# GpSimd's sums of the output weights in 256-column operations, and three of seven low parts moved from VectorE to GpSimd

## The chip, the cores and the metric

One core of one Trainium2 chip runs the whole program. The metric is the device time of one execution in microseconds; a kernel's time is the median of its runs.

## The reference

The block is x + attention(xn) w_o + ffn(xn), with xn the layer norm of x, for 4 sequences of 512 tokens of 1024 values. What the change touches is the output projection of the attention, whose input is 2048 tokens by 4096 values (32 heads of 128) and whose weight w_o is 4096 by 1024:

```
qkv = hidden_states @ w_qkv            # 32 query heads, 8 key and value heads of 128
attn = softmax(scores * scale + bias)  # causal, bias = -slope * sqrt(distance)
out  = einsum(attn, v).reshape(B, S, 32 * 128)
return out @ w_o                       # the stage of this case
```

## The kernel before

Every fp32 product is made of three matmuls of split numbers: an operand is stored as a high part (`_hi`, type fp32r) and a low part (`_lo`, the number less its high part), and `product` (L643) issues high by high (L645), high by low (L646) and low by high (L647). ScalarE makes high parts (`high`, L892), VectorE or GpSimd the low parts (`low`, L1127; GpSimd's own, L592).

The first half of the span projects q, k, v and the ffn and stores them in DRAM. The second, from about 1215 us, is a loop over 128 units of attention (a sequence and a head), 4 units to a set, 2 sets to a group, so 16 groups of 8 units. Four engines run the same loop, each with its own written-out order. In unit n TensorE does the scores of n, then the transposes and the attention product of unit n-1 (`scores`, `transposes`, `attend`), and between them three or four "fills": parts of the output projection of an earlier set.

The output projection of a set is a block product of 2 by 2 blocks with seven products in place of eight. Its 14 parts are 2 tiles of 7 steps. A step multiplies an activation operand (`op_hi`, `op_lo`) with a weight operand `wo[:, step]`, a high and a low plane of 128x1024. VectorE adds each result to `acc` (`add_fill`, L1395). A fill waits for its weight's low part in the first tile of a group (L853), for its activation's low part (L854), and, as two PSUM banks alternate, for the addition of the fill before the last (L856).

The weights of a group are made once, in the four units n = 8g+2 to 8g+5 (`making`). Steps 0, 1 and 6 are blocks as loaded into `wo_raw`; steps 4, 2, 3 and 5 are sums and differences that GpSimd makes in `wo_sums` (L595), one 128x1024 operation each: step 4 in unit 8g+2, step 2 in 8g+3, steps 3 and 5 in 8g+4. `OUT_SPLITS` says in which unit they are split: 0 and 1 in 8g+3, 2, 3 and 4 in 8g+4, 5 and 6 in 8g+5. ScalarE makes the high parts at the end of its unit (L1114), VectorE the low parts at the end of its own (L1446), so ahead of its `maxima` of the next unit. `maxima` (L1364) frees the score banks and gives ScalarE its first exponential. In units 8g+4 to 8g+7 `bias_of` (L1353) follows it on VectorE.

GpSimd also makes the sums of activation operands (`out_sum`, L586) and their low parts (`out_low`, L592), all in operations of 128x256. In unit 8g+5 (`at_once`) it makes two sums and the low parts of parts 1, 2 and 3, which TensorE uses in the same unit; ScalarE makes their high parts ahead of that unit's exponentials, and for part 2 waits for GpSimd's sum. SyncE loads the next group's `wo_raw` in unit 8g+7, after all low parts of this one (L435).

Of the kernel before, what the change touches and what calls it, by code (L numbers as in the profile page):

```python
# [7 lines left out]
ALU = mybir.AluOpType  # L8
ACT = mybir.ActivationFunctionType
AX = mybir.AxisListType  # L10
F32 = mybir.dt.float32
# [33 lines left out]
STEPS = 7  # L45
# [14 lines left out]

OUT_SPLITS = ((), (0, 1), (2, 3, 4), (5, 6))
WO_SUMS_IN = ((4,), (2,), (3, 5), ())
GROUPS = SETS // 2


def block_program(nc, x, w_all, w_o, w_ag, w_lora, gate_b, consts, out):
    with ExitStack() as ctx:
        base = 16512

        def at(name, offset, shape, dt=F32):  # L70
            return nc.alloc_sbuf_tensor_at(name, shape, dt, offset=base + offset)

        def sem(name):
            return ctx.enter_context(nc.semaphore(name))
# [45 lines left out]
        k = at("k", 8 * K, [P, 2, 2, SEQ], F32R)  # L120
# [9 lines left out]
        wo = at("wo", 76 * K, [P, STEPS, 2, 1024], F32R)  # L130
# [73 lines left out]
        s_wo_sum = sem("s_wo_sum")  # L204
        s_wo_hi = sem("s_wo_hi")
        s_wo_lo = sem("s_wo_lo")
        s_bias = sem("s_bias")
        s_scores = sem("s_scores")
        s_neg_max = sem("s_neg_max")
# [18 lines left out]
        def number(pr, m, st):  # L228
            return (pr * MATRICES + m) * STEPS + st
# [36 lines left out]
        def stores_h(pr, m, i):  # L266
            return stored_h(pr, m, i) + 16 * 3 * (4 * pr + (min(i, 4) if m == VALUES else 4))

        def stores_r(pr, m, i):
            return stored(pr, m, i) + 16 * 3 * (2 * pr + (min(i, 2) if m == VALUES else 2))  # L270
# [57 lines left out]
        def making(n):  # L328

            group, since = (n - 2) // (2 * G), (n - 2) % (2 * G)  # L330
            return (group, since) if n >= 2 and group < GROUPS and since < G else (None, None)

        def out_splits(n):

            group, since = making(n)
            return [] if group is None else [(group, i) for i in OUT_SPLITS[since]]

        def out_sums_in(n):

            group, since = making(n)  # L340
            return [] if group is None else [(group, i) for i in WO_SUMS_IN[since]]

        WO_SUMS = (4, 2, 3, 5)

        def summed(group, step):
            return len(WO_SUMS) * group + WO_SUMS.index(step) + 1

        def used(group, step):

            return PARTS * (2 * group - 1) + STEPS + step + 1  # L350

        def wo_source(step):

            return {0: wo_raw[0][:, :], 1: wo_raw[1][:, :], 6: wo_raw[3][:, :], 4: wo_raw[2][:, :],
                    5: wo_raw[1][:, :]}.get(step, wo_sum[:, step, 1])
# [4 lines left out]
        def _(sp):  # L360
# [51 lines left out]
            def out_block(group, i):  # L412

                half, pair = i // 2, i % 2
                head = group % KV_HEADS * G + 2 * pair
                sp.dma_start(wo_raw[i][:, :].rearrange("p (h c) -> p h c", h=2),
                             w_o[bass.ds(head * P, 2 * P), half * 512:(half + 1) * 512].rearrange("(h p) c -> p h c", p=P)
                             ).then_inc(s_wo_raw[i], 16)

            def out_weights(n):  # L420

                if n in (1, 2):
                    sp.wait_ge(s_bank, 4 * TOTAL)
                    for i in ((0, 2), (1, 3))[n - 1]:
                        out_block(0, i)
                if n in range(3, 7):

                    sp.wait_ge(s_store_h, stores_h(2, VALUES, 0))
                    sp.wait_ge(s_store_a, stores_r(2, VALUES, 0))
                    sp.wait_ge(s_store_b, stores_r(2, VALUES, 0))  # L430
                    for tt in ((0, 2), (1, 3), (4, 6), (5, 7))[n - 3]:
                        sp.dma_start(acc[:, tt, :], acc_s[bass.ds(tt * P, P), :]).then_inc(s_acc_in[tt], 16)
                group = n // (2 * G)
                if n % (2 * G) == G + 3 and group + 1 < GROUPS:
                    sp.wait_ge(s_wo_lo, STEPS * (group + 1))  # L435
                    sp.wait_ge(s_wo_sum, len(WO_SUMS) * (group + 1))
                    for i in range(4):
                        out_block(group + 1, i)
# [21 lines left out]
            for n in range(UNITS):  # L460
                pr, g, b, h = unit(n)
                s = n // G
# [24 lines left out]
        def _(pool):  # L487
# [107 lines left out]
            def wo_sums(group, step):  # L595

                a11, a12, a21, a22 = (r[:, :] for r in wo_raw)
                to, first, second, op = {4: (a21, a11, a21, ALU.subtract), 2: (wo_sum[:, 2, 1], a22, a21, ALU.subtract),
                                         5: (a12, a12, wo_sum[:, 2, 1], ALU.subtract),
                                         3: (wo_sum[:, 3, 1], wo_sum[:, 2, 1], a11, ALU.add)}[step]  # L600
                if step == 4:
                    pool.wait_ge(s_wo_raw[0], 16 * (group + 1))
                    pool.wait_ge(s_wo_raw[2], 16 * (group + 1))
                if step == 2:
                    pool.wait_ge(s_wo_raw[3], 16 * (group + 1))
                if step in (2, 3) and group:
                    pool.wait_ge(s_fill, used(group, step))
                elif step in (2, 3):
                    pool.wait_ge(s_bank, 4 * TOTAL)
                if step != 4:  # L610
                    pool.wait_ge(s_wo_sum, summed(group, 4 if step == 2 else 2))
                if step == 5:
                    pool.wait_ge(s_wo_lo, STEPS * group + 2)
                nc.gpsimd.tensor_tensor(to, first, second, op).then_inc(s_wo_sum, 1)

            for n in range(UNITS + G + 1):
                at_once, later = shaped(n)
                s, c = n // G - 1, n % G
                for group, step in out_sums_in(n) if c == 0 else ():
                    wo_sums(group, step)  # L620
                if c == 0 and at_once + later:
                    pool.wait_ge(s_at_raw, G * s + 2)
                    for tile, k in OUT_SUMS[0:2]:
                        out_sum(s, tile, k)
                if at_once:
                    pool.wait_ge(s_at_raw, G * (s + 1))
                    for tile, k in OUT_SUMS[2:4]:
                        out_sum(s, tile, k)
                for part in at_once:
                    out_low(*part)  # L630
                if at_once:
                    out_sum(s, *OUT_SUMS[4])
                if c == 2 and later:
                    for tile, k in OUT_SUMS[5:8]:
                        out_sum(s, tile, k)
                for part in later:
                    out_low(*part)
                for group, step in out_sums_in(n) if c != 0 else ():
                    wo_sums(group, step)

        @block.tensor
        def _(pe):
# [205 lines left out]
            def fill_in(s, tile, k):  # L848

                part = tile * STEPS + k  # L850
                f = PARTS * s + part
                if s % 2 == 0 and tile == 0:
                    pe.wait_ge(s_wo_lo, STEPS * (s // 2) + k + 1)  # L853
                pe.wait_ge(s_op_lo, f + 1)  # L854
                if f >= 2:
                    pe.wait_ge(s_acc, f - 1)  # L856
                for kt in range(2):
                    cols = slice(kt * 512, (kt + 1) * 512)
                    last = product(fill[f % 2][:, :], (op_hi[:, part, kt, :], op_lo[:, part, kt, :]),
                                   (wo[:, k, 0, cols], wo[:, k, 1, cols]), kt == 0 and k in STARTS, kt == 1)  # L860
                last.then_inc(s_fill, 1)
# [256 lines left out]
        def _(dve):  # L1118
# [278 lines left out]
            def out_split(group, step):  # L1397

                dve.wait_ge(s_wo_hi, STEPS * group + step + 1)
                if step == 2:  # L1400
                    dve.wait_ge(s_wo_sum, len(WO_SUMS) * (group + 1))
                low(wo[:, step, 1], wo_source(step), wo[:, step, 0], s_wo_lo)
# [10 lines left out]
            for pr in range(PAIRS):  # L1413
                operands(pr)
                for m in range(MATRICES):
                    for st in range(STEPS):
                        n = number(pr, m, st)
# [16 lines left out]
            for n in range(UNITS + G + 1):  # L1434
                todo = fills(n)
                if 1 <= n < UNITS:
                    maxima(n)
                for f in todo[:1]:
                    add_fill(*f)
                if 1 <= n <= UNITS:  # L1440
                    transposed(n - 1)
                if n < UNITS:
                    inverses(n)
                for f in todo[1:]:
                    add_fill(*f)
                for part in out_splits(n):  # L1446
                    out_split(*part)


def constants():  # L1450
# [40 lines left out]
```

## Time and profile before

| | us |
|---|---|
| median of 3 runs | 2588.23 (2588.20 to 2589.75) |
| the profiled execution | 2589.15 |
| its span | 2587.4 |
| TensorE matmuls busy | 2440.0 (94%) |
| VectorE busy | 1627.0 (63%) |
| ScalarE busy | 1440.8 (56%) |
| GpSimd busy | 842.5 (33%) |

The busy times are of the whole span. In a timeline row the columns are start, duration, engine, line, operation, operands with shapes and count; in brackets stands how long the engine was idle before it and what released it.

### The profile page before, as it was taken

To read this page: it belongs to the slowest core of one execution; us is meant where nothing else is said; L and a number is where in the kernel's file an instruction comes from. 1 tells how busy PE (TensorE), PEld (TensorE's weight loads), DVE (VectorE), ACT (ScalarE), POOL (GpSimd) and SP (SyncE) were. 2 spreads that over 40 slices of the span, in tenths; PEclk is the share of its full clock that TensorE was granted. 3 is DMA by queue.
4 is the path that set the end of the run, shared out by engine and by line. 5 is a ranking of instruction groups with operands and counts; after the bars stand their busy time and mean duration, and the time that the engine had idled before them with its cause. 6 is when DMAs were issued, how large, how long until landed. Compare 5 with 4: busy or idle time off the path is not lost.

```text
span 2587.4 us, 34927 instructions
## 1 busy us (share of the span) xinstructions
PE 2440.0 (94%) x12128; PEld 2059.5 (80%) x12128; DVE 1627.0 (63%) x2905; ACT 1440.8 (56%) x3131; POOL 842.5 (33%) x966
## 2 busy tenths in 40 slices
PE   5999999996999999998899999999999999999998
PEld 4787888885777888886788878887888878888787
DVE  6657455555757355564676677667766777667765
ACT  4432133334523133334777777777776777777774
POOL 3211000002221000001355455544554455544544
PEclk9999999998999999999999999999999999999999
DMA  4536354464355444546422323132335231332221
GB/s 148 179 131 222 114 209 157 159 221 166 119 167 195 146 150 175 195 157 229 165 101 84 117 98 115 66 115 98 115 131 187 102 111 59 122 115 98 81 99 74
DMA packets 94703, 355.25 MB, mean 137 GB/s; under 512 B 8874, under 2 KB 9018, under 8 KB 85569
## 3 DMA queue, kind: packets, MB, share of 16 engines
q1 hardware_dynamic: 62480, 233.43, 25.1%
q0 software_dynamic: 32048, 119.60, 13.3%
q8 instruction: 97, 1.59, 0.2%
q14 instruction: 78, 0.63, 0.1%
HBM read 235.02 MB, written 117.97 MB: 136 GB/s over the span
## 4 chain that ended last, share of the span: by engine, by line
PE 78%; DVE 10%; issue 6%; ACT 3%; DMA 1%; POOL 1%; SPq 0%; DVEq 0%; ACTq 0%; POOLq 0%
PE ps L645 25%; PE ps L646 24%; PE ps L647 24%; PE ps L832 4%; DVE wo L1127 3%; DVE probs L1364 2%; DVE acc L1395 2%; ACT res_hi L892 1%; DVE stats L1141 1%; ACT rows L921 1%; DVE w_lo L1127 0%; DVE res_b L1127 0%; DMA lora_lo<-lora_s 0%; DVE res_a L1217 0%; DVE res_a L1127 0%
## 5 line engine op out<-in xcount | busy, mean ns | idle before, releaser
L892 ACT ACTIVATE w_hi<-raw 128x1024 fp32r<-128x1024 f32 x196 | 207.0, 1059 | 560.3 <-PE ps L647 440.4
L1127 DVE TENSOR_TENSOR w_lo<-raw,w_hi 128x1024 fp32r<-128x1024 f32 x196 | 239.1, 1223 | 358.5 <-ACT w_hi L892 358.4
L1395 DVE TENSOR_TENSOR acc<-ps,acc 128x512 f32<-128x512 f32 x448 | 298.0, 686 | 228.6 <-issue 207.9
L645 PE MATMUL ps<-x_hi,w_hi 128*128 128x512 f32 x1120 | 436.5, 390 | 0.0
L646 PE MATMUL ps<-x_lo,w_hi 128*128 128x512 f32 x1120 | 436.0, 389 | 0.0
L647 PE MATMUL ps<-x_hi,w_lo 128*128 128x512 f32 x1120 | 435.8, 389 | 0.0
L645 PE MATMUL ps<-wo,op_hi 128*128 128x512 f32 x896 | 368.4, 411 | 69.2 <-DVE acc L1395 55.4
L1032 ACT ACTIVATE probs<-probs,neg_max 128x512 f32<-128x512 f32 (+3 forms) x512 | 283.4, 565 | 212.5 <-DVE neg_max L1364 212.5
L647 PE MATMUL ps<-wo,op_lo 128*128 128x512 f32 x896 | 357.5, 399 | 0.0
L646 PE MATMUL ps<-wo,op_hi 128*128 128x512 f32 x896 | 355.9, 397 | 0.0
L1364 DVE CUSTOM_DVE_ANT_0 probs<-ps,bias 128x512 f32<-128x512 f32 (+3 forms) x512 | 220.4, 485 | 96.0 <-PE ps L647 93.9
L645 PEld LDWEIGHTS ps<-wo,op_hi 128*128 128x128 f32 x896 | 170.4, 190 | 108.5 <-issue 82.7
L592 POOL TENSOR_TENSOR op_lo<-op_raw,op_hi 128x256 fp32r<-128x256 f32 x256 | 189.6, 751 | 198.9 <-ACT op_hi L892 188.7
L1046 ACT ACTIVATE probs<-probs,row_inv 128x128 f32<-128x128 f32 (+3 forms) x512 | 245.5, 555 | 9.8 <-DVE row_inv L1376 9.8
L647 PEld LDWEIGHTS ps<-x_hi,w_lo 128*128 128x128 f32 x1120 | 210.4, 188 | 44.0
L645 PEld LDWEIGHTS ps<-x_hi,w_hi 128*128 128x128 f32 x1120 | 210.4, 188 | 43.7
L646 PEld LDWEIGHTS ps<-x_lo,w_hi 128*128 128x128 f32 x1120 | 210.4, 188 | 43.2
L518 POOL DMA_DIRECT2D qk_s<-res_hi x40 | 30.1, 753 | 656.3 <-ACT res_hi L892 645.5
L592 POOL TENSOR_TENSOR op_lo<-at_raw,op_hi 128x256 fp32r<-128x256 f32 x192 | 140.6, 739 | 305.2 <-ACT op_hi L892 209.6
L892 ACT ACTIVATE pt_hi<-ps 128x512 fp32r<-128x512 f32 (+1 forms) x384 | 173.2, 523 | 98.5 <-PE ps L832 98.3
L1127 DVE TENSOR_TENSOR pt_lo<-ps,pt_hi 128x512 fp32r<-128x512 f32 (+1 forms) x384 | 206.5, 592 | 26.1 <-ACT pt_hi L892 26.1
L647 PEld LDWEIGHTS ps<-wo,op_lo 128*128 128x128 f32 x896 | 171.0, 191 | 38.8
(156 smaller groups left out, 4997.3 us busy)
## 6 DMA issues: line engine op xcount, KB each, us to landing
raw<-w_all SPq DMA_DIRECT2D x70, 1024.0 KB, 5.2
q<-qk_s SPq DMA_DIRECT2D x128, 512.0 KB, 3.3
qk_s<-res_hi POOLq DMA_DIRECT2D x40, 1024.0 KB, 4.6
wo_raw<-w_o SPq DMA_DIRECT2D x64, 512.0 KB, 5.7
qk_s<-res_a POOLq DMA_DIRECT2D x20, 1024.0 KB, 9.1
qk_s<-res_b POOLq DMA_DIRECT2D x20, 1024.0 KB, 5.3
k<-qk_s SPq DMA_DIRECT2D x32, 512.0 KB, 5.8
v<-v_s SPq DMA_DIRECT2D x32, 512.0 KB, 7.9
```

The lines of the kernel that those rows point to most:

```text
L518: pool.dma_start(qk_s[b, first:first + 4, :, level, :].rearrange("h p c -> p h c"), source).then_inc(signal, 16)
L592: nc.gpsimd.tensor_tensor(op_lo[:, part], op_source(s, part), op_hi[:, part].bitcast(F32), ALU.subtract).then_inc(s_op_lo, 1)
L645: pe.matmul(to, st_hi, mv_hi, start=start, stop=False, skip_group_check=True)
L646: pe.matmul(to, st_hi, mv_lo, start=False, stop=False, skip_group_check=True)
L647: return pe.matmul(to, st_lo, mv_hi, start=False, stop=stop, skip_group_check=True)
L832: last = pe.transpose(to[:, c * P:(c + 1) * P], probs[:, n % 2, OFF[i] + j * P:OFF[i] + (j + 1) * P], ident[:, :])
L892: nc.scalar.activation(to, source, ACT.Copy).then_inc(signal, 1)
L1032: nc.scalar.activation(tile, tile, ACT.Exp, bias=neg_max[:, i:i + 1], scale=-1.0, accum_out=row_sum[:, i:i + 1]).then_inc(s_exp, 1)
L1046: last = nc.scalar.activation(tile, tile, ACT.Copy, scale=row_inv[:, i:i + 1])
L1127: nc.vector.tensor_tensor(to, source, high.bitcast(F32), ALU.subtract).then_inc(signal, 1)
L1364: nc.vector.tensor_tensor_reduce(out=probs[:, n % 2, OFF[i]:OFF[i] + (i + 1) * P], in0=score_bank[i], in1=bias[:, h, SEQ - (i + 1) * P:SEQ ...
L1395: nc.vector.tensor_tensor(to, fill[f % 2][:, :], to, ALU.add).then_inc(s_acc, 1)
```

## The change

`wo_sums` makes each sum in four operations of 256 columns, and signals after the last. The low parts of the weight operands 4, 5 and 6 are made by GpSimd, also in four operations each, at the end of its unit (after that unit's activation work), with a semaphore of their own, `s_wo_low`. VectorE keeps 0 to 3. TensorE and SyncE wait for the semaphore that fits.

```diff
+BY_POOL = (4, 5, 6)
+BY_DVE = STEPS - len(BY_POOL)
...
-                    sp.wait_ge(s_wo_lo, STEPS * (group + 1))
+                    sp.wait_ge(s_wo_lo, BY_DVE * (group + 1))
+                    sp.wait_ge(s_wo_low, len(BY_POOL) * (group + 1))
...
                 if step == 5:
-                    pool.wait_ge(s_wo_lo, STEPS * group + 2)
-                nc.gpsimd.tensor_tensor(to, first, second, op).then_inc(s_wo_sum, 1)
+                    pool.wait_ge(s_wo_lo, BY_DVE * group + 2)
+                for i in range(4):
+                    cut = slice(i * 256, (i + 1) * 256)
+                    last = nc.gpsimd.tensor_tensor(to[:, cut], first[:, cut], second[:, cut], op)
+                last.then_inc(s_wo_sum, 1)
+
+            def out_split(group, step):
+
+                pool.wait_ge(s_wo_hi, STEPS * group + step + 1)
+                for i in range(4):
+                    cut = slice(i * 256, (i + 1) * 256)
+                    last = nc.gpsimd.tensor_tensor(wo[:, step, 1, cut], wo_source(step)[:, cut],
+                                                   wo[:, step, 0, cut].bitcast(F32), ALU.subtract)
+                last.then_inc(s_wo_low, 1)
...
                 for group, step in out_sums_in(n) if c != 0 else ():
                     wo_sums(group, step)
+                for group, step in out_splits(n):
+                    if step in BY_POOL:
+                        out_split(group, step)
...
                 if s % 2 == 0 and tile == 0:
-                    pe.wait_ge(s_wo_lo, STEPS * (s // 2) + k + 1)
+                    if k in BY_POOL:
+                        pe.wait_ge(s_wo_low, len(BY_POOL) * (s // 2) + k - BY_DVE + 1)
+                    else:
+                        pe.wait_ge(s_wo_lo, BY_DVE * (s // 2) + k + 1)
...
-                for part in out_splits(n):
-                    out_split(*part)
+                for group, step in out_splits(n):
+                    if step not in BY_POOL:
+                        out_split(group, step)
```

## Rows read from the trace of the kernel before

**Rows 1.** The page: busy time of each engine; the chain that ended last, by engine.
```profile
PE 2440.0 (94%) x12128; PEld 2059.5 (80%) x12128; DVE 1627.0 (63%) x2905; ACT 1440.8 (56%) x3131; POOL 842.5 (33%) x966
...
PE 78%; DVE 10%; issue 6%; ACT 3%; DMA 1%; POOL 1%; SPq 0%; DVEq 0%; ACTq 0%; POOLq 0%
```

**Rows 2.** Waits, 1390 to 2587 us: waiter, releaser: us in total, times, longest.
```profile
PE ps L645 <- DVE acc L1395: 51.4, 27, 3.3
```

**Rows 3.** Timeline of TensorE: rows with idle time before them, and one group's transposes.
```profile
1763.13 0.47 PE L645 MATMUL ps<-wo,op_hi 128*128 128x512 f32 x1 [2.09 <-issue]
...
2093.27 0.77 PE L645 MATMUL ps<-wo,op_hi 128*128 128x512 f32 x1 [3.29 <-DVE acc L1395]
...
2101.34 1.25 PE L832 MATMUL ps<-ident,probs 128*128 128x128 f32 x10
2103.42 0.47 PE L645 MATMUL ps<-wo,op_hi 128*128 128x512 f32 x1 [0.83 <-issue]
...
2115.98 0.47 PE L645 MATMUL ps<-wo,op_hi 128*128 128x512 f32 x1 [0.53 <-DVE acc L1395]
```

**Rows 4.** Timeline of VectorE in the same group, from the end of unit 8g+3.
```profile
2084.90 4.84 DVE L1127 TENSOR_TENSOR wo<-wo_raw,wo 128x1024 fp32r<-128x1024 f32 x2
...
2091.42 1.10 DVE L1353 TENSOR_SCALAR bias<-dist,slopes 128x512 f32<-128x512 f32 x1
...
2097.67 2.36 DVE L1127 TENSOR_TENSOR wo<-wo_sum,wo 128x1024 fp32r<-128x1024 f32 x2 [0.72 <-ACT wo L892]
...
2110.38 2.68 DVE L1127 TENSOR_TENSOR wo<-wo_raw,wo 128x1024 fp32r<-128x1024 f32 x2
```

**Rows 5.** The first two alone, by form, around 2085 and 2089: busy us, mean ns.
```profile
L1127 DVE TENSOR_TENSOR wo<-wo_raw,wo 128x1024 fp32r<-128x1024 f32 x1 | 1.5, 1507 | 0.0
...
L1127 DVE TENSOR_TENSOR wo<-wo_raw,wo 128x1024 fp32r<-128x1024 f32 x1 | 3.4, 3405 | 0.0
```

**Rows 6.** Tile wo, all groups: ns shortest/median/longest, first and last start.
```profile
L1127 DVE TENSOR_TENSOR wo<-wo_sum,wo x32: 1216/1222/1227, 1248.9 to 2522.0; 128x1024 fp32r<-128x1024 f32 x32
```

**Rows 7.** Timeline of GpSimd in the same group.
```profile
2082.91 2.42 POOL L614 TENSOR_TENSOR wo_sum<-wo_raw,wo_raw 128x1024 f32<-128x1024 f32 x1
2085.48 3.19 POOL L614 TENSOR_TENSOR wo_sum<-wo_sum,wo_raw 128x1024 f32<-128x1024 f32 x1
2089.89 2.35 POOL L614 TENSOR_TENSOR wo_raw<-wo_raw,wo_sum 128x1024 f32<-128x1024 f32 x1 [1.23 <-DVE wo L1127]
...
2100.09 2.55 POOL L586 TENSOR_TENSOR op_raw<-at_raw,op_raw 128x256 f32<-128x256 f32 x2 [5.01 <-ACT at_raw L892]
2102.59 0.73 POOL L592 TENSOR_TENSOR op_lo<-at_raw,op_hi 128x256 fp32r<-128x256 f32 x1
...
2117.68 1.43 POOL L592 TENSOR_TENSOR op_lo<-at_raw,op_hi 128x256 fp32r<-128x256 f32 x2 [6.83 <-PE ps L647]
...
2127.34 0.74 POOL L592 TENSOR_TENSOR op_lo<-at_raw,op_hi 128x256 fp32r<-128x256 f32 x1
2128.03 0.74 POOL L592 TENSOR_TENSOR op_lo<-op_raw,op_hi 128x256 fp32r<-128x256 f32 x1
```

**Rows 8.** Timeline of ScalarE in the same group.
```profile
2094.76 1.92 ACT L1046 ACTIVATE probs<-probs,row_inv 128x128 f32<-128x128 f32 x4 [0.56 <-DVE row_inv L1376]
...
2098.49 1.05 ACT L892 ACTIVATE wo<-wo_raw 128x1024 fp32r<-128x1024 f32 x1
...
2101.85 0.72 ACT L892 ACTIVATE op_hi<-op_raw 128x256 fp32r<-128x256 f32 x2 [1.33 <-POOL op_raw L586]
...
2108.61 2.00 ACT L892 ACTIVATE wo<-wo_raw 128x1024 fp32r<-128x1024 f32 x2
```

**Rows 9.** Busy time by window; after POOL's comes the granted clock.
```profile
2094.00:2097.00 3.00, 3.00 (x11) 2.37 (x10) 2.00 (x5) 2.44 (x6) 0.73 (x1) 0.62 0.00 0
```

**Rows 10.** Timeline of SyncE's DMA queue in the same group.
```profile
2113.10 1.92 SPq L416 DMA_DIRECT2D wo_raw<-w_o  x4
2115.06 0.57 SPq L470 DMA_DIRECT2D k<-qk_s  x1
```

More of the change, by code:

```diff
@@ L206, in block_program @@
         s_wo_lo = sem("s_wo_lo")
+        s_wo_low = sem("s_wo_low")
         s_bias = sem("s_bias")
```

## The prediction

> **What bounds the kernel now.** I read the page first (busy times, then the chain), the waits of the attention half, and then the timelines of one group's four weight units on all engines. The page shows TensorE busy for 94% of the span and on 78% of the chain, VectorE on 10% [rows 1]. So the question is only where TensorE stands idle. The waits give one large item, TensorE on VectorE's addition, 51.4 us after 1390 us [rows 2]. The timeline of TensorE places it [rows 3]: in each group it idles at three places. A, in unit 8g+4: 3.29 us (14 groups; the last has 2.16, the first none of this kind). B, in 8g+5: 0.83 us. C, in 8g+6: 0.53 us. In the other five units the work is TensorE's own, so a group's period changes only by what happens between A and C.
>
> A comes from VectorE. The low parts of weights 0 and 1 take 4.84 us [rows 4], 1507 and 3405 ns [rows 5], where undisturbed ones take 1222 [rows 6]. Each ends 1.2 us after a GpSimd sum ends: GpSimd's step 2 runs 2082.91 to 2085.33, step 3 2085.48 to 2088.67 and itself takes 3.19 instead of about 2.4 [rows 7]. The two engines take turns, an instruction at a time. VectorE's bias (1.10 us) then ends just after GpSimd's step 5 does (2092.24) [rows 4, 7]; the addition behind it releases TensorE at 2093.27 [rows 3].
>
> A to B is always 10.15 us (2093.27 to 2103.42), and it is not TensorE's. VectorE's delay holds ScalarE, whose high part 4 ends at 2099.54 [rows 8]. GpSimd makes two activation sums (2100.09 to 2102.64), ScalarE waits 1.33 us for the first, and the low part of part 1 ends at 2103.32, when TensorE starts [rows 3, 7, 8]. TensorE's own work has slack there, which hides a low clock: after A it is granted 0.62 of its clock, 1.2 GHz for much of the stretch (2094 to 2097) [rows 9]. In 13 of 15 groups it is low for some 3 us or more after A. In the two where it isn't, B shows 2.1 us idle in place of 0.6 to 0.8 in nine groups (one in between, none visible in three) [rows 3]. So a low stretch costs about 1.3 to 1.5 us, up to 2.1, and B swallows it today. From B to C TensorE has no such slack.
>
> **The sums in pieces.** GpSimd's 128x256 operations are 0.74 us each but start 0.69 apart (2127.34, 2128.03) [rows 7]. Four are 2.8 us against 2.4, +0.4 for each of four sums. Steps 4 and 2 end with time to spare. What is gained is at A. The first low part arrives at 2084.90, as the third piece ends; it runs to 2086.15 instead of 2086.41. The fourth piece takes its turn (0.6 us), the second low part ends at 2087.87 instead of 2089.74: 1.87 earlier. The bias then waits for one piece of step 3, 0.2 us instead of 0.6. So VectorE is 2.2 to 2.3 us earlier, and TensorE's wait shrinks from 3.29 to about 1.0. Bounds: nothing, if VectorE can't get in between adjacent pieces, to 2.7, all of the 4.84 - 2.43 and more of the bias. I take 2.2, because the row at 2100.09 (two 256-column operations in 2.55 us beside a VectorE low part) shows turns after single operations.
>
> The Trainium skill, "SBUF — State Buffer", section "Who interferes with whom", says that a VectorE instruction with two SBUF inputs contends with GpSimd's reads, and that who issues first keeps the shared ports for the whole instruction. By that the piece length is what VectorE waits for; by a shared bandwidth it would gain nothing and the group would lose 2.2 us more. The trace agrees with the first (3405 ns beside one 2.4 us sum).
>
> ScalarE's normalise (2094.76) waits for VectorE, so it and the three high parts behind it move by 2.2, and high part 4 ends at 2097.34, call it T [rows 8]. Its other input, step 3, ends by 2091.0.
>
> **Low part 4 on GpSimd.** On VectorE it goes away behind 2 and 3, which run 2.36 us from T-1.87 before [rows 4]. That time isn't late there: what is late at B is GpSimd. GpSimd has the new work in its path: it waits for T, then 4 x 0.7 = 2.8 us, and only then the two sums (1.4 us) and the low part of part 1 (0.7 us), in program order. Two collisions come on top: step 5 ends about 2093.9, so the low part of part 0 delays VectorE's low parts 2 and 3, and the latter holds the port until T+0.8 (0.65 us more than without); the bias takes 0.4 during the pieces. TensorE then starts part 1 at T + 0.15 + 2.8 + 0.65 + 0.4 + 2.1 + 0.12 = T+6.2 = 2103.57. Before it was T+3.88. B costs 2.35 us against 2.2 gained: +0.15 against 2103.42. Without the collisions it would be -0.9, with the bad end at A +2.4. ScalarE's wait for the sum, 1.33 us, grows to some 3.7 and delays the unit's first exponential by 0.25.
>
> **The clock after B.** TensorE works 7.7 us at full clock between its release at A and the end of the transposes (2093.27 to 2102.59 less 1.6 lost to the low clock). Released at 2091.0 it is done at 2098.7, then idles until 2103.57: 4.9 us, more than the 3.29 after which the clock fell in 13 of 15. The low stretch now lies where nothing hides it. I take 1.5 us; bounds 0 (no fall) and 2.1 or a little more.
>
> **Low parts 5 and 6.** VectorE loses 2.68 us ahead of the maxima of unit 8g+6 [rows 4]; the idle at C goes, with the restart 0.6 us. GpSimd starts low part 5 after the high part (2108.61 + 1.05, now +0.25), ends it at 2112.85 and low part 6 at 2115.65, or 2116.05 with the bias between. TensorE wants number 6 at 2115.5 if its clock stayed up, at about 2117 if it fell: in the forecast the wait costs nothing, otherwise it is late next by up to 0.6 us. GpSimd's next work, sums and low parts for unit 8g+7, starts 3.5 us later and meets 6.83 us of idle in that queue [rows 7]. SyncE waits for all low parts: the weight loads and the load of k behind them, at 2113.10 [rows 10], go 3 us later; k is for unit 8g+8, whose scores come after all of 8g+7's work, and the weights for 8g+10. Hidden.
>
> **Sum.** A loaded group: +0.15 + 1.5 - 0.6 = +1.05 us. Fifteen of them: +15.8. The first group's sums ran before its low parts (nothing to gain but the bias), so it pays B almost whole: +2. Together +18. The profiled execution of 2589.15 us would be 2607, the median of 2588.23 so 2606.
>
> **Rivals.** (1) The clock stays up, or low part 6 eats the difference: +0.15 - 0.6, and up to 0.6 of wait back, 0 us a group, 2588 to 2592. For it: two groups of 15 kept their clock after 3.29 us. Against: 4.9 us is longer. (2) Faster: GpSimd's work at B meets no collision (VectorE's low part 3 finishes first, the bias falls elsewhere), -0.9 in place of +0.15, and the clock stays up or falls briefly: -0.8 a group, 2576. For it: all my times at B come from a phase of 0.5 us. Against: low part 3 starts after high part 3 and must last 1.2 us, past T. (3) Much slower: VectorE isn't let in between adjacent pieces at A. Then sum 2 and 3 hold it as before and 0.4 longer, and B's 2.35 stands unpaid: +2.4 + 0.4 + 1.5 - 0.6 = +3.7 a group, 2644. It decides from the first low part's duration: over 2 us says so. Against it stands the row at 2100.09, and only the reverse case (VectorE's turn) is well seen. The Trainium skill speaks against the change: "Perfetto Trace Analysis", section "Optimizing Scalar/DVE Operations", says that moving work between VectorE and GpSimd might not help, for their shared port. Here that is the collision term, 1.05 us a group at B; no row shows these pieces themselves.
>
> **Chances.** Forecast 0.53 (2596 to 2624, by the bounds of the clock and of half a microsecond at A and B), rival 1 0.16, rival 2 0.20, rival 3 0.11. A measurement tells 0.2% (5 us) from no change. Slower: forecast and rival 3, 0.64; same: most of rival 1, 0.14; faster: rival 2 and the rest, 0.22. The range reaches into rivals 1 and 2 below and stops short of rival 3: 2577 to 2627.
>
> **What would show it.** Low parts 0 and 1 together near 3.0 us (over 4.5: rival 3). TensorE's idle at A near 1, at B near 4.5 to 5, and a granted clock of about 0.6 just behind B and none low behind A. ScalarE waiting 3 to 4 us for a sum in unit 8g+5. GpSimd's low part 4 in 2.8 to 3.9 us. Idle at C gone. The forecast is wrong if B's idle is under 3 us, or if the clock stays up behind it.

## The result, and the profile after

The changed kernel takes 2602.64 us (median of 5 runs, 2600.86 to 2603.92) against 2588.56 (5 runs, 2588.20 to 2590.07) for the kernel before on the same chip: ratio 1.0052, 95% interval 1.0038 to 1.0067. It is slower by 14 us; forecast were 18. The profiled execution took 2603.18 us, its span is 2601.2, 13.8 longer than before.

The page of the changed kernel, busy times and then the chain by engine, beside [rows 1]:

```profile
PE 2444.5 (94%) x12128; PEld 2066.1 (79%) x12128; DVE 1547.2 (59%) x2857; ACT 1443.5 (55%) x3131; POOL 1013.7 (39%) x1350
...
PE 88%; DVE 4%; issue 4%; ACT 2%; POOL 1%; DMA 1%; SPq 0%; DVEq 0%; ACTq 0%; POOLq 0%
```

VectorE is 80 us less busy and GpSimd 171 more. VectorE fell from 10% of the chain to 4%, yet the end came later.

The waits from 1390 us on (waiter, releaser: us in total, times, longest), to be read beside [rows 2]:

```profile
PE ps L665 <- issue: 60.1, 15, 4.4
...
PE ps L665 <- DVE acc L1418: 11.6, 14, 0.9
```

TensorE's wait for VectorE's addition, A, shrank from 51.4 us to 11.6. In its place stand 60.1 us with no releaser named, 15 times: B, once in each of the 15 loaded groups (those behind the first). The timeline of TensorE in the group of [rows 3] (idle time before a row in brackets):

```profile
2099.75 0.47 PE L665 MATMUL ps<-wo,op_hi 128*128 128x512 f32 x1 [0.88 <-DVE acc L1418]
...
2106.50 1.25 PE L852 MATMUL ps<-ident,probs 128*128 128x128 f32 x10
...
2111.86 0.77 PE L665 MATMUL ps<-wo,op_hi 128*128 128x512 f32 x1 [4.11 <-issue]
2112.42 0.63 PE L666 MATMUL ps<-wo,op_hi 128*128 128x512 f32 x1
```

A idles 0.88 us instead of 3.29. From A to B it is 12.11 us instead of 10.15, with 4.11 us of idle in it. No row of C has idle time any more. Behind B the matmuls of 512 columns take 0.6 to 0.8 us and not 0.39. VectorE in the same group (the low parts of steps 0 and 1, the bias, the low parts of steps 2 and 3, the next bias), beside [rows 4]:

```profile
2093.80 2.93 DVE L1150 TENSOR_TENSOR wo<-wo_raw,wo 128x1024 fp32r<-128x1024 f32 x2
...
2098.40 0.60 DVE L1376 TENSOR_SCALAR bias<-dist,slopes 128x512 f32<-128x512 f32 x1
...
2104.15 2.54 DVE L1150 TENSOR_TENSOR wo<-wo_sum,wo 128x1024 fp32r<-128x1024 f32 x2 [1.76 <-ACT wo L915]
...
2108.36 0.57 DVE L1376 TENSOR_SCALAR bias<-dist,slopes 128x512 f32<-128x512 f32 x1
```

GpSimd, beside [rows 7]: the sums for steps 2, 3 and 5, the low part of step 4, and behind it the activation sums and low part on which TensorE waits at B:

```profile
2091.82 3.82 POOL L621 TENSOR_TENSOR wo_sum<-wo_raw,wo_raw 128x256 f32<-128x256 f32 x4
2095.79 3.79 POOL L621 TENSOR_TENSOR wo_sum<-wo_sum,wo_raw 128x256 f32<-128x256 f32 x4
2099.54 2.83 POOL L621 TENSOR_TENSOR wo_raw<-wo_raw,wo_sum 128x256 f32<-128x256 f32 x4
...
2106.09 3.43 POOL L629 TENSOR_TENSOR wo<-wo_raw,wo 128x256 fp32r<-128x256 f32 x4 [1.62 <-ACT wo L915]
2109.48 1.59 POOL L591 TENSOR_TENSOR op_raw<-at_raw,op_raw 128x256 f32<-128x256 f32 x2
2111.03 0.73 POOL L597 TENSOR_TENSOR op_lo<-at_raw,op_hi 128x256 fp32r<-128x256 f32 x1
```

ScalarE, beside [rows 8]: high part 4, and the activation's high parts after the wait for GpSimd's sum.

```profile
2104.97 1.04 ACT L915 ACTIVATE wo<-wo_raw 128x1024 fp32r<-128x1024 f32 x1
...
2110.30 0.72 ACT L915 ACTIVATE op_hi<-op_raw 128x256 fp32r<-128x256 f32 x2 [3.29 <-POOL op_raw L591]
```

So B is a chain through three engines: ScalarE ends high part 4 at 2106.01, GpSimd's low part 4 follows to 2109.52, two sums and one low part to 2111.76, and TensorE starts at 2111.86.

Two windows of 3 us, behind A and behind B (columns as in [rows 9]; the granted clock follows POOL's time). The kernel before had 0.62 behind A [rows 9] and the full clock behind B.

```profile
2099.80:2102.80 3.00, 3.00 (x16) 2.46 (x16) 2.58 (x6) 2.96 (x11) 3.00 (x5) 1.00 0.00 0
2111.90:2114.90 3.00, 3.00 (x7) 2.44 (x8) 1.84 (x5) 3.00 (x11) 1.96 (x4) 0.50 0.02 5
```

The low stretch has moved from behind A to behind B: 0.50 of the clock is the 1.2 GHz level. The clock fell behind B in all 15 loaded groups. In 8 of them the 3 us from B on were granted 0.50, as here. In the other 7 they were granted 0.61 to 0.69, because the fall came later. From 1300 us on, 140 matmuls of 512 columns take over 0.55 us; before it was 90.

A group lasted 84.7 to 84.95 us before (start to start of its first low part; once 85.77). Now it lasts 85.0 us where 7 or 8 of those matmuls ran at the low level, and 85.6 to 86.0 where 11 or 12 did; once 87.75, with 2.48 us of idle before scores that waited for q:

```profile
1967.97 0.47 PE L665 MATMUL ps<-k,q 128*128 128x512 f32 x1 [2.48 <-issue]
```

The kernel before in the same unit:

```profile
1960.09 0.47 PE L645 MATMUL ps<-k,q 128*128 128x512 f32 x1 [0.78 <-issue]
```

Up to the first loaded group the kernel loses 2.5 us, over 14 group periods 9.6 (0.69 each), and behind the last 1.7: together 13.8.

### The profile page after: what moved, and what is told of

It is laid out like the page before. It is cut to its first block, busy times and chain, and to the rows that moved or that the text cites. A ratio compares the mean times of both kernels' runs of the same rounds, so it can differ in the third digit from the quotient of the medians.

```text
span 2601.2 us, 35263 instructions
## 1 busy us (share of the span) xinstructions
PE 2444.5 (94%) x12128; PEld 2066.1 (79%) x12128; DVE 1547.2 (59%) x2857; ACT 1443.5 (55%) x3131; POOL 1013.7 (39%) x1350
## 4 chain that ended last, share of the span: by engine, by line
PE 88%; DVE 4%; issue 4%; ACT 2%; POOL 1%; DMA 1%; SPq 0%; DVEq 0%; ACTq 0%; POOLq 0%
PE ps L665 28%; PE ps L666 27%; PE ps L667 27%; PE ps L852 5%; DVE stats L1164 1%; ACT rows L944 1%; ACT res_hi L915 1%; DVE w_lo L1150 0%; DVE acc L1418 0%; DMA k<-qk_s 0%; DVE res_a L1240 0%; DVE res_a L1150 0%; DVE res_b L1240 0%; PE ps L747 0%; ACT w_hi L915 0%
## 5 line engine op out<-in xcount | busy, mean ns | idle before, releaser
L665 PE MATMUL ps<-wo,op_hi 128*128 128x512 f32 x896 | 374.6, 418 | 78.0 <-issue 61.7
L667 PE MATMUL ps<-wo,op_lo 128*128 128x512 f32 x896 | 363.8, 406 | 0.0
L666 PE MATMUL ps<-wo,op_hi 128*128 128x512 f32 x896 | 363.4, 406 | 0.0
```

What stands on the lines that cost most here:

```text
L665: pe.matmul(to, st_hi, mv_hi, start=start, stop=False, skip_group_check=True)
L666: pe.matmul(to, st_hi, mv_lo, start=False, stop=False, skip_group_check=True)
L667: return pe.matmul(to, st_lo, mv_hi, start=False, stop=stop, skip_group_check=True)
```

## The experiments

The theory: the pieces gain at A; low part 4 loses more at B, because GpSimd's activation work stands behind it in the same queue, and because TensorE's longer idle there is followed by the low clock. The first rival: the pieces are themselves a loss or nothing, and moving VectorE's work pays. The second: the loss is the engines' contention, wherever the low parts stand. All ratios are to the kernel before, which took about 2589.7 us on each chip used here and 2588.56 beside the changed kernel. So a difference of plain times between one of these kernels and the changed one can be off by about 1 us.

**pieces: the sums in pieces, no low part moved.**

```diff
-BY_POOL = (4, 5, 6)
+BY_POOL = ()
```

SyncE's wait on `s_wo_low`, which then nobody signals, goes too.

> Only the sums in 256-column pieces; all seven low parts stay on VectorE. Theory (pieces earn at A, low part 4 on GpSimd spends it at B, the clock behind B costs the rest): idle at A 0.9 us, A to B again 10.1 to 10.2 us, idle at C still about 0.5, so 2.4 us a loaded group: 2552 us if the clock stays up behind B, about 2575 if it falls there. Rival (the pieces themselves cost, by more issue and more turns): 2588 us or above.

Measured: 2560.83 us, ratio 0.9889 (0.9873 to 0.9906). TensorE at A, B and C of one group:

```profile
1661.14 0.47 PE L664 MATMUL ps<-wo,op_hi 128*128 128x512 f32 x1 [0.87 <-DVE acc L1417]
...
1671.15 0.47 PE L664 MATMUL ps<-wo,op_hi 128*128 128x512 f32 x1 [2.00 <-issue]
...
1683.95 0.47 PE L664 MATMUL ps<-wo,op_hi 128*128 128x512 f32 x1 [0.33 <-DVE acc L1417]
```

A has the 0.87 us of the changed kernel, from A to B it is 10.01 us (before 10.15), and only 29 slow matmuls are left. The half of the change that gains is this one: 29 us. It lies between the two values expected, since the clock fell behind B in 4 of the 14 groups whose B idles 2.0 us. Before, B's idle was shorter only because the low clock behind A filled it.

**moved_whole: the low parts moved, the sums as before.**

```diff
-                for i in range(4):
-                    cut = slice(i * 256, (i + 1) * 256)
-                    last = nc.gpsimd.tensor_tensor(to[:, cut], first[:, cut], second[:, cut], op)
-                last.then_inc(s_wo_sum, 1)
+                nc.gpsimd.tensor_tensor(to, first, second, op).then_inc(s_wo_sum, 1)
```

> Only the move of low parts 4, 5 and 6 to GpSimd; the sums stay whole. Theory: idle at A 3.3 us as before, A to B 12.1 us, idle at B near 3 us with a low clock behind it in many groups: +2.0 +1.0 to 1.6 -0.6 a group, 2625 to 2634 us. Rival (the pieces cost, the move is neutral): 2585 to 2592 us.

Measured: 2621.83 us, ratio 1.0125 (1.0110 to 1.0140). A and B:

```profile
1504.53 0.47 PE L662 MATMUL ps<-wo,op_hi 128*128 128x512 f32 x1 [3.29 <-DVE acc L1415]
...
1516.46 0.70 PE L662 MATMUL ps<-wo,op_hi 128*128 128x512 f32 x1 [3.90 <-issue]
```

A is as before and A to B is 11.9 to 12.0 us: the loss at B has nothing to do with the pieces of the sums. The moved low parts alone cost 32 us, the pieces alone gain 29. The two do not add up to the change's +14; on top of the pieces the move costs 42. What differs most is where the clock falls: with A's long idle kept, the clock fell behind A in 12 of the 14 groups with that idle. Where it fell there alone, B idles 1.3 to 2.5 us, which takes up the low stretch, and the group lasts 86.1 to 86.4 us. In 5 of the 14 the clock fell behind B, and all but one of those groups last 87.2 (the other has a long idle before scores). In the changed kernel it falls behind B every time. A fall behind B in many groups was expected here too, and the time is 3 us below that range.

**pieces_56: as changed, but low part 4 stays on VectorE.**

```diff
-BY_POOL = (4, 5, 6)
+BY_POOL = (5, 6)
```

> The change, but low part 4 goes back to VectorE; 5 and 6 stay on GpSimd. Theory: A 0.9 us, A to B near 10.2 us, C's idle gone: 3 us a group less than before, 2543 us with the clock up, up to 2566 if it falls behind B. Rival (low parts 5 and 6, with the loads of SyncE behind them, are what costs): no better than 2595 us.

Measured: 2555.90 us, ratio 0.9870 (0.9855 to 0.9884), 46.7 us below the changed kernel, from one low part of the three. A to B is 10.01 us again, C has no idle, 16 matmuls are slow. Low parts 5 and 6 gain, about 5 us (the intervals of the two kernels just overlap, but a group lasts 81.97 us against 82.4 to 83.6 in "pieces"); low part 4 alone does the harm. Against the second rival: the moved instructions are of one kind and contend alike, and two of three gain. One row spoils some of it (the clock fell behind it, and this group lasts 89.14 us):

```profile
1944.44 0.76 PE L665 MATMUL ps<-k,q 128*128 128x512 f32 x1 [4.19 <-issue]
```

**filled: the changed kernel with TensorE kept busy while it waits at B.** Ahead of the wait 16 more matmuls (`FILLER`) of 512 columns run on key tiles, and their results are used nowhere.

```diff
+                if s % 2 == 0 and part == 1:
+                    if f >= 2:
+                        pe.wait_ge(s_acc, f - 1)
+                    keys = key_sets[:, (s + 1) % 2, 0, :]
+                    for _ in range(FILLER):
+                        pe.matmul(fill[f % 2][:, :], keys[:, 0:P], keys, start=True, stop=True,
+                                  skip_group_check=True)
```

> The changed kernel, with 16 matmuls of 128x512 on key tiles put ahead of TensorE's wait at B, into a bank that the next fill starts anew; their results are used nowhere. Theory: TensorE is busy through most of the 4.1 us, the clock stays at 2.4 GHz behind B, 1.6 to 2.2 us a group less, of which the wait for low part 6 takes back up to 0.6: 2577 to 2588 us. Rival (the clock is a symptom, C is bound by GpSimd's low parts 5 and 6): unchanged, 2600 to 2604 us.

Measured: 2581.80 us, ratio 0.9971 (0.9959 to 0.9983), 20.8 us below the changed kernel although TensorE does more. TensorE at B, and the window behind it:

```profile
2096.11 3.90 PE L880 MATMUL ps<-k 128*128 128x512 f32 x16
2100.53 0.47 PE L666 MATMUL ps<-wo,op_hi 128*128 128x512 f32 x1 [0.52 <-issue]
```
```profile
2100.60:2103.60 3.00, 3.00 (x14) 2.48 (x15) 2.10 (x5) 3.00 (x11) 1.98 (x4) 1.00 0.00 0
```

The wait isn't shortened (A to B 12.18 us), only its consequence is gone: full clock behind B in every loaded group, and from 1300 us on no matmul of 512 columns over 0.55 us instead of 140. The window holds 14 matmuls; behind B of the changed kernel it held 7. The clock behind B costs 20.8 / 15 = 1.4 us a group. (The term was 1.5.)

**halves_512 and eighths_128: "pieces" with other sizes,** to see whether VectorE's turns go by the length of a piece.

```diff
-                for i in range(4):
-                    cut = slice(i * 256, (i + 1) * 256)
+                for i in range(2):
+                    cut = slice(i * 512, (i + 1) * 512)
```

> As 'pieces' (all low parts on VectorE), but the sums in two operations of 512 columns. Theory (VectorE waits out one GpSimd operation per turn): low parts 0 and 1 take near 3.9 us together, between 4.84 whole and 2.92 in pieces of 256, idle at A near 1.9 us, 2570 to 2576 us. Rival (VectorE gets in between any two operations at the moment it asks, the length doesn't matter): 2.9 us and 2561 us.

Measured: 2574.28 us, ratio 0.9940 (0.9925 to 0.9955), low parts 0 and 1 take 3.88 us (3.9 expected), idle at A is 2.22 us: between 3.29 (whole) and 0.87 (quarters). For the other, `range(8)` and slices of 128:

> As 'pieces', with eight operations of 128 columns. Theory: VectorE's turn comes a little sooner (2.7 to 2.8 us for the two), but each operation has a fixed cost, so a sum gets longer still: 2558 to 2566 us, no use beyond 256. Rival (the gain goes on in proportion): under 2555 us.

Measured: 2590.90 us, ratio 1.0010 (1.0001 to 1.0020). This is 25 us above the expected range; its ten runs spread from 2585.59 to 2599.57, and the trace is of the fastest. All groups of the tile wo_sum on GpSimd, and TensorE in unit 8g+5:

```profile
L620 POOL TENSOR_TENSOR wo_sum<-wo_sum,wo_raw x128: 450/459/647, 1221.7 to 2510.9; 128x128 f32<-128x128 f32 x128
```
```profile
1672.80 0.76 PE L664 MATMUL ps<-wo,op_hi 128*128 128x512 f32 x1 [3.19 <-DVE wo L1149]
```

A 128-column operation costs 0.46 us, not half of 0.74. A sum becomes 3.4 to 3.6 us, up to 5.4 with turns given away, and the weights' low parts come late (3.19 us of idle, on VectorE's). A itself was down to 0.78 us. Of the three lengths tried 256 is the best: below it the fixed cost of an operation eats what the turns gain.

**change_sync and p56_sync: SyncE's order.** In a unit, SyncE issues the group's weight loads, which wait for all low parts, ahead of the reads and writes of `acc`; q of the next unit is behind both. Both kernels exchange the two:

```diff
-                out_weights(n)
                 results(n)
+                out_weights(n)
```

> The changed kernel with one edit, SyncE's stores and reloads of the accumulator ahead of its wait for the low parts. Theory: the idle time of 2.48 us once in the half goes, and the one of the kernel before at the same place with it: 2.5 to 4 us less, 2599 us. It was left out of the prediction, which called SyncE's delay hidden. Rival: no difference.

> As 'pieces_56', with SyncE's stores and reloads of the accumulator ahead of its wait for the low parts. Theory: the one idle time of 4.19 us in the middle of the half (the change has 2.48 us there), which is a q load queued behind those reloads, goes: 3 to 4.5 us less than pieces_56, about 2552 us. Rival (it is DRAM or the stores themselves): no difference.

Measured: the change with it 2599.20 us, ratio 1.0034 (1.0022 to 1.0045), 3.4 us less than without; pieces_56 with it 2546.52 us, ratio 0.9837 (0.9822 to 0.9851), 9.4 less. The intervals of the first pair overlap and those of the second just don't, but in both traces the long idle before scores is gone. So the 2.48 us at 1967.97 are SyncE's. For pieces_56, 3 to 4.5 us were expected. The profiled executions differ by 11.9: 7.2 in the group with the long idle (4.19 us and the low clock behind it) and 1.4 in the last group, where the clock no longer falls. The remaining 3.2 lie ahead of the first group's low parts and are unexplained. SyncE's queue in the changed kernel, the row after the third being q:

```profile
1950.34 1.92 SPq L420 DMA_DIRECT2D wo_raw<-w_o  x4
1952.30 2.09 SPq L447 DMA_DIRECT2D out<-acc  x4
...
1961.08 4.26 SPq L461 DMA_DIRECT2D acc<-acc_s  x4
1965.38 5.10 SPq L476 DMA_DIRECT2D q<-qk_s  x2
```

Counted from the start of their group's first low part (1920.09 here, 1914.18 before) the weight loads go out at 30.25 us and not at 28.21, and this q at 45.29 and not at 43.21: both 2.1 us later.

**low4_later: the low parts on GpSimd, but 4 behind the activation work of unit 8g+5,** so that nothing is queued behind it that TensorE waits for; with SyncE's new order.

```diff
                 if at_once:
                     out_sum(s, *OUT_SUMS[4])
+                    if making(n)[0] is not None:
+                        out_split(making(n)[0], 4)
...
-                    if step in BY_POOL:
+                    if step in BY_POOL and step != 4:
```

> The change with low part 4 moved on GpSimd's queue from the end of unit 8g+4 to behind unit 8g+5's sums and low parts 1 to 3, and with SyncE's stores and reloads of the accumulator ahead of its wait for the low parts. Theory: the place in the queue was the loss, not the engine: A 0.9 us, A to B 9.1 to 9.5 us (GpSimd's sums no longer collide with VectorE's low part 4 either), C's idle nearly gone: 2538 to 2548 us. Rival (three low parts are more than GpSimd can carry between B and C, number 6 is late by as much): 2556 us or above.

Measured: 2564.08 us, ratio 0.9897 (0.9881 to 0.9913). It is 16 us above the expected range. B came out as expected (A to B 9.2 us, idle 1.2), C didn't. GpSimd, VectorE and TensorE of one group:

```profile
1674.96 5.61 POOL L629 TENSOR_TENSOR wo<-wo_raw,wo 128x256 fp32r<-128x256 f32 x8
```
```profile
1676.85 4.68 DVE L1378 TENSOR_SCALAR bias<-dist,slopes 128x512 f32<-128x512 f32 x1
```
```profile
1682.28 0.47 PE L667 MATMUL ps<-wo,op_hi 128*128 128x512 f32 x1 [2.28 <-DVE acc L1420]
```

VectorE's bias lasts 4.68 us, alone 0.5 to 0.6: asked for at 1676.85, it ends at 1681.53, one microsecond behind GpSimd's run of eight adjacent pieces (1680.57). So it is in 11 of 15 groups; the addition behind it keeps TensorE waiting. In the other four nothing holds it, although it comes at the same point of a piece (0.47 to 0.49 us in):

```profile
1345.82 0.53 DVE L1378 TENSOR_SCALAR bias<-dist,slopes 128x512 f32<-128x512 f32 x1
```

A loaded group without the hold lasts 81.6 us, though C still idles 0.8 us, now for low part 6 as the rival has it. With the hold it lasts 83.2, and 84.6 in the six groups where the clock falls behind C as well. The hold and that clock are the miss. The Trainium skill, "SBUF — State Buffer", section "Who interferes with whom", has whoever issues first keep the ports that VectorE and GpSimd share for the whole instruction, while the other blocks; it says so of VectorE's 2-port modes. A piece is 0.7 us, so the hold here spans some six instructions, and the measurement goes beyond the rule.

**low4_gaps: the same, each piece waiting for the semaphore of the one before.**

```diff
-                last.then_inc(s_wo_low, 1)
+                    last.then_inc(s_wo_low, 1)
+                    if i < 3:
+                        pool.wait_ge(s_wo_low, 4 * (len(BY_POOL) * group + step - BY_DVE) + i + 1)
```

The other waits on `s_wo_low` are multiplied by 4.

> As 'low4_later', where VectorE's bias of unit 8g+6 was held 4.7 us through GpSimd's run of adjacent pieces; each piece of a low part now signals, and the next waits for it. Theory (VectorE gets in only if GpSimd's next operation isn't already waiting to start; a gap lets it in): bias under 1.3 us everywhere, idle at C 0.8 us or less, about 2548 us. Rival (what decides is when in a piece the request comes, gaps or not): still some 4 us in many groups, 2560 us or above.

Measured: 2558.82 us, ratio 0.9879 (0.9864 to 0.9893), 11 above what was expected. The bias of unit 8g+6 takes 0.49 us in all 15 groups, so with a wait between the pieces the hold does not occur. (The bias now also comes later in a piece, 0.67 to 0.72 us in, so more than the wait is different.) But eight pieces take 6.50 us instead of 5.61, and now low part 6 is what TensorE waits for:

```profile
1675.71 6.50 POOL L629 TENSOR_TENSOR wo<-wo_raw,wo 128x256 fp32r<-128x256 f32 x8
```
```profile
1682.26 0.50 PE L669 MATMUL ps<-wo,op_hi 128*128 128x512 f32 x1 [1.47 <-POOL wo L629]
```

**p56_dve4_later: p56_sync with VectorE's low part 4 moved back in VectorE's own order,** behind the inverses of unit 8g+5. Where it stood, it ran beside GpSimd's two sums, which took 2.40 us in p56_sync:

```profile
1661.50 2.40 POOL L591 TENSOR_TENSOR op_raw<-at_raw,op_raw 128x256 f32<-128x256 f32 x2 [2.11 <-ACT at_raw L915]
```

```diff
+                if making(n)[1] == 3:
+                    out_split(making(n)[0], 4)
...
-                    if step not in BY_POOL:
+                    if step not in BY_POOL and step != 4:
```

> As 'p56_sync', with low part 4 still on VectorE but in unit 8g+5, behind the inverses instead of ahead of that unit's maxima. Theory: at B neither engine has it in the way (in p56_sync it delays GpSimd's sums and VectorE's maxima): A to B 9.2 us instead of 10.0, 0.8 us a group less, 2533 to 2540 us. Rival (VectorE's additions come too late for the fill of part 3, or C is bound by low part 6 anyway): 2546 us or above.

Measured: 2530.46 us, ratio 0.9773 (0.9757 to 0.9789): the fastest of all, 2.5 us below the expected range. A and B:

```profile
1649.47 0.47 PE L665 MATMUL ps<-wo,op_hi 128*128 128x512 f32 x1 [0.86 <-DVE acc L1418]
...
1658.69 0.47 PE L665 MATMUL ps<-wo,op_hi 128*128 128x512 f32 x1 [1.18 <-issue]
```

A to B is 9.22 us, and a group lasts 80.9. GpSimd's two sums last 1.61 us, 0.79 less, which is what A to B has lost:

```profile
1656.30 1.61 POOL L591 TENSOR_TENSOR op_raw<-at_raw,op_raw 128x256 f32<-128x256 f32 x2 [2.11 <-ACT at_raw L915]
```

## Why the prediction was right

The forecast was slower by 18 us by one mechanism, a gain at A that B takes back and more; it is slower by 14, by this mechanism. Step by step:

- **The sums in pieces** were right. Low parts 0 and 1 take 2.93 us (3.0 forecast), A idles 0.88 (1.0). VectorE takes its turn between adjacent pieces there. halves_512 shows the dependence on length.
- **Low part 4 on GpSimd**: the place and the queue were right, as pieces_56 shows by undoing it. The term was mis-sized: from A to B it costs 1.96 us and not 2.35. With a gain at A of 2.41 and not 2.2, A and B together are -0.46 and not +0.15. High part 4 ends 6.26 us after A, as expected (6.34), but TensorE starts 5.85 us later and not 6.2: low part 4 took 3.43 us where 3.85 were counted. Both its collisions are there and were sized too high: the first piece, beside VectorE's low part 3, takes 1.20 us instead of 0.74 (0.46 where 0.65 were counted), the last, which meets the bias, 0.92 (0.18 where 0.4 were). ScalarE's wait is 3.29 (3.7 forecast), B's idle 4.11 (4.9).
- **The clock after B** was right: it falls in every loaded group. What the periods leave for it is 0.69 + 0.46 + 0.53 (C) less 0.12 for SyncE (next item), about 1.6 us: 1.2 where 7 or 8 matmuls are slow and 1.9 where 11 or 12 are. The same sum for change_sync, which has no long group, gives 1.5, and filled 1.4. The term was 1.5. One reading behind it was slightly off: the clock fell after 3.29 us in 12 groups of 14. The thirteenth fall is the last group's, after only 2.16.
- **Low parts 5 and 6** were right at C: its idle is gone and number 6 isn't waited for. What was wrong is "Hidden", the step on SyncE. I moved the weight loads and k and followed these to their users, but not q, which stands behind them in the same queue and is needed in the very next unit. It cost 2.48 us of idle once, where the kernel before has 0.78. The one long group is 2.75 us over the others now and was 1.0 over them before, so SyncE's share of the loss is about 1.7 us, or 0.12 a group. (The 3.4 us of change_sync take away both.)
- **The sum**: +0.69 us a period instead of +1.05, with SyncE's share in it, 14 of them, and 4.2 at both ends where 2 plus one more group, 3.1, were counted. So the periods were put 5 us too high and the ends 1 us too low. In a period A and B together were 0.6 us too dear. Against that, SyncE's 0.12 was missing, and clock and C were each under 0.1 too cheap.
- **The rivals**: the first and second failed by the clock, which never stayed up behind B. The second was half right in its other part: its smaller collisions put A and B at -0.9, and the measured -0.46 lies between that and the forecast. The third failed at A, where its test (a first low part over 2 us) came out the other way. But what it describes, VectorE kept out by adjacent pieces, exists in this kernel: in low4_later, with the bias as its victim.

## What to carry to other kernels

Before work is moved to a less busy engine, look at what stands behind it in that engine's queue, and who waits for that: of three equal low parts two gained 5 us and the one ahead of TensorE's next input lost 47. The busy share said nothing on this (GpSimd 33%), and the same work moved back in VectorE's own order gained 16 us. A change in two parts should be run part by part: here the total of +14 us hid one part of -29. And the parts need not add up: the move costs 32 us alone and 42 on top of the pieces, mostly since the clock falls at another place.

## What the runs showed of the hardware that was not expected

- **Adjacent GpSimd operations can keep VectorE out over several of them** (bias 4.68 us in low4_later), yet between the sums VectorE got in after one (2.93 us for two low parts). In the changed kernel and pieces_56 a bias that was ready within 0.1 us of a piece's start was held for one piece (1.01 to 1.12 us); at 0.42 to 0.44 us into a piece it wasn't held (0.57 to 0.60). In low4_later it came 0.47 to 0.50 us into a piece and was held for the whole run in 10 groups, and not at all in 4 with the same point and the same operations (0.53 to 0.56). With a semaphore wait between the pieces it took 0.49 us in 15 of 15. So neither the kinds of the two operations nor the point in the piece, as far as the trace resolves it, decides alone; what does stays open.
- **Operations of GpSimd have a fixed cost**: 1024 columns 2.35 to 2.42 us, 256 columns 0.74 (0.70 start to start), 128 columns 0.46.
- **The clock followed the length of the idle stretch, not strictly**: after 4.1 to 4.4 us it fell in 15 of 15 groups, after 3.29 us in 12 of 14 [rows 3], after 2.2 us (A in halves_512) in 8 of 14, after 2.0 us (B) in 4 of 14 in "pieces" and in none in pieces_56. Matmuls on unused data in the gap kept it up and gained 20.8 us, less than removing the gap does.
